# Local attention in a transformer block: the softmax division moved ahead of the transposes, the value product made transposed, and the second half of each tile finished one tile later

## The chip, the cores and the metric

The kernel runs on one core of one Trainium2 chip. The metric is the device time of one execution, in microseconds (us). A core has five engines that each work through a list of instructions in order and wait for each other by semaphores: TensorE (PE in the profile; PEld is its weight load), VectorE (DVE), ScalarE (ACT), GpSimd (POOL) and SyncE (SP, which only issues DMAs here). The on-chip memory SBUF is called `store` in the profile's names, and the eight PSUM banks that TensorE writes are `bank`.

## What is computed

Eight sequences of 512 tokens, 128 wide, pass through four residual blocks: a Mamba-2 block, a two-layer transformer with local attention (call 0), a small attention with distance decay, and the same two-layer transformer again (call 1). The change touches the local attention, which runs four times (2 calls x 2 layers). Its reference, cut to what matters:

```python
q, k, v = split(shift_token(x) @ wqkv)            # 8 heads of 64
q, k = l2norm(q) * qs, l2norm(k) * ksc
q, k = rotary_xpos(q, k)
# windows of 64 queries; each sees its own 64 keys and the 64 before
sim = einsum('bhwid,bhwjd->bhwij', bq * 8, bk)    # masked to a band
attn = softmax(sim)
out = einsum('bhwij,bhwjd->bhwid', attn, bv)
x = x + out @ wo                                  # 512 -> 128
```

After it comes a feed-forward part with a layer norm and a GELU gate.

## The kernel before

**Tiles and stages.** In each layer the eight sequences q are taken one after another, and each is four tiles j of 128 tokens: 32 tiles a layer, 128 in all. A tile passes through a pipeline that is written out by hand, per engine, in a function `attention_sequence`. In the step of tile j, the engines work on several tiles at once:

- TensorE: scores of tile j (`scores`, lines 622 and 629, into banks 3 and 4), the product with the values of tile j-1 (`weigh_values`, 654, into bank 7), the projection of the values of tile j+2 (`project_v`, 600, bank 2), the transposes of the rotated q and k of tile j+1 (`qk_transpose`, 607, banks 5 and 6), the transposes of the attention output of j-1 (`o_transpose`, 662), the transposes of the probabilities (`prob_transpose`, 642, banks 5 and 6), the projection of q and k of tile j+3 (`project_qk`, 593, banks 0 and 1), the output projection of j-1 (`project_out`, 668) and the transpose of an input tile (`x_transpose`, 587).
- VectorE: row maxima (`maxima`, 987), division of the output of j-1 by the sums (`take_o`, 998), the rotary products of tile j+2 (`rotate`, 969 and 974, once for q and once for k), their square sums (981, 983), the reciprocals of the sums (`inverse_sums`, 992), the residual add (`add_out`, 1005).
- ScalarE: squares (822), exponentials of the even and odd heads (`exps`, 844, e = 0 and e = 1), and the copies out of PSUM: values (`copy_v`, 828), q and k (`copy_qkT`, 833 and 835), output (`copy_oT`, 855), probabilities (`copy_pT`, 850).
- GpSimd: adds the two rotary products (`add_turned`, 1134), raises the square sums to the power -1/2 (`inverse_norms`, 1140), and scales q and k (`normalize`, 1149).

**What sets the order.** Nothing but the order of the calls on each engine and the semaphores. Three waits matter below. `project_qk(n, i)` writes bank i and waits on `rot_done` until `rotate` has read tile n-1 out of that bank: the wait is for 8q+2j+i+1 with a credit of 2, so i of tile n needs rotation i of tile n-1. `x_transpose` writes bank 2 and waits on `v_ready` until the values of tile j+2 of this sequence have been copied out of it. `scores` waits on `qT_ready` until both q and k of its tile are copied.

Of the kernel before, what the change touches and what calls it, by code (L numbers as in the profile page):

```python
# [17 lines left out]
ALU = mybir.AluOpType  # L18
# [3 lines left out]
P = 128  # L22
# [115 lines left out]
def hybrid_block(nc, a, out):  # L138
# [3 lines left out]
    with ctx:  # L142
# [52 lines left out]
        onorm = mem.take(INNER)  # L195
        oT = mem.take(PAIRS, P)
        nmax = mem.take(2, PAIRS)
        psums = mem.take(H)
        pinv = mem.take(H)
# [84 lines left out]
        clip_done, pinv_done, fstat_done, feps_done = sem("clip_done"), sem("pinv_done"), sem("fstat_done"), sem("feps_done")  # L284
# [7 lines left out]
        pT_done, pT_ready, o_done, onorm_ready = sem("pT_done"), sem("pT_ready"), sem("o_done"), sem("onorm_ready")  # L292
        oT_done, oT_ready = sem("oT_done"), sem("oT_ready")
# [288 lines left out]
        def transformer_pe(pe, call):  # L582
# [62 lines left out]
            def weigh_values(q, j):  # L645
# [3 lines left out]
                for e in range(2):  # L649
                    pe.wait_ge(pT_ready, n2 + e + 1)  # L650
                    for b in range(PAIRS):
                        h = 2 * b + e
                        for half, v in ((0, VA), (1, V)):
                            last = nc.tensor.matmul(bank[7][half * WIN:(half + 1) * WIN, h * DH:(h + 1) * DH],  # L654
                                                    probT[:, e, b, half * WIN:(half + 1) * WIN], v[:, j, h * DH:(h + 1) * DH],
                                                    start=True, stop=True, skip_group_check=True)
                last.then_inc(o_done, 1)

            def o_transpose(q, j):
                pe.wait_ge(onorm_ready, 4 * q + j + 1)  # L660
                for b in range(PAIRS):
                    last = nc.tensor.transpose(bank[7][:, b * P:(b + 1) * P], onorm[:, b * P:(b + 1) * P], ident)  # L662
                last.then_inc(oT_done, 1)
# [8 lines left out]
            def attention_sequence(q, before, more, ff_ahead=False):  # L672
                for j in range(TPS):
                    prev = (q, j - 1) if j else (q - 1, TPS - 1)
                    has_prev = before or j > 0
# [4 lines left out]
                    if has_prev:  # L680
                        weigh_values(*prev)
                    if more or j < 2:
                        project_v(*((q, j + 2) if j < 2 else (q + 1, j - 2)), more or j == 0)
                    if has_next:
                        qk_transpose(*nxt)
                    if has_prev:
                        o_transpose(*prev)
                    prob_transpose(q, j, 0, has_next)
                    if has_ahead:
                        project_qk(*ahead, 0)  # L690
                    if has_prev:
# [1585 lines left out]
```

## Time and profile before

| what | before |
|---|---|
| median of 3 runs | 2251.19 us (2249.34 to 2251.57) |
| the profiled execution's own time | 2245.52 us |
| its span, first to last instruction | 2243.7 us |
| busy: PE, DVE, ACT, POOL | 95%, 72%, 66%, 75% |
| granted TensorE clock, mean | 0.992 |
| attention stages | 302.9 to about 575 us, 655 to 924, 1545 to 1818, 1898 to 2167 |

A row of the timeline gives start, length, engine, line, operation, and in brackets the idle time just before it and what ended it. Rows are merged when the same line follows itself (x4 is four instructions). An engine takes its next instruction a little before the last one's recorded end, so the distance between starts ("pitch") is a little less than a length.

### The profile page before, as it was taken

The numbers are of one execution on the slowest core, as the hardware profiler recorded it, in microseconds if no ns is written. First come the engines' busy times: TensorE is split into PE (matmuls) and PEld (weight loads), VectorE is DVE, ScalarE is ACT, GpSimd is POOL, SyncE is SP. The second block draws the span as 40 slices with busy tenths as digits, with TensorE's granted clock in tenths as the row PEclk, the third lists the DMA queues.
The fourth block names the chain that finished last, engine by engine and source line by source line (L and its number), as shares of the span: only waits on it lengthen the run. The fifth ranks groups of instructions, "written<-read, shape, count | busy, mean of one in ns | idle before, by whom it ended". The sixth has DMA issues, their size and how long they took to land.

```text
span 2243.7 us, 54540 instructions
## 1 busy us (share of the span) xinstructions
PE 2140.1 (95%) x19744; PEld 1477.6 (66%) x19760; DVE 1613.2 (72%) x3907; ACT 1475.8 (66%) x4130; POOL 1677.2 (75%) x1710
## 2 busy tenths in 40 slices
PE   6999889999999999899999999999999989999998
PEld 4767657777567777556666666565777756777765
DVE  6777568887467777667767777777888756777765
ACT  3666458888458888536656556566888854888862
POOL 7877788998158888448777787778898824888852
PEclk9999989999999999999999999999999999999999
DMA  4000001112111122121111121111111211111211
GB/s 118 1 1 1 7 21 44 35 32 49 48 29 40 33 46 46 43 71 50 49 54 35 48 58 50 44 27 23 42 25 44 46 45 31 37 34 40 47 31 51
DMA packets 121371, 88.42 MB, mean 39 GB/s; under 512 B 85560, under 2 KB 102160, under 8 KB 118800
## 3 DMA queue, kind: packets, MB, share of 16 engines
q1 hardware_dynamic: 118544, 82.69, 15.2%
q8 instruction: 159, 2.61, 0.5%
q10 hardware_dynamic: 2560, 2.24, 0.4%
q14 instruction: 108, 0.88, 0.1%
HBM read 30.38 MB, written 8.39 MB: 17 GB/s over the span
## 4 chain that ended last, share of the span: by engine, by line
PE 65%; DVE 7%; POOL 5%; SPq 5%; issue 3%; DMA 2%; ACT 1%; POOLq 0%; DVEq 0%
PE bank L1328 11%; PE bank L593 8%; PE bank L1339 5%; PE bank L1319 5%; PE bank L607 5%; PE bank L654 4%; PE bank L642 4%; PE bank L629 4%; PE bank L600 4%; PE bank L668 4%; SPq L466 4%; POOL store L1140 3%; PE bank L720 2%; PE bank L662 2%; POOL store L1149 2%
## 5 line engine op out<-in xcount | busy, mean ns | idle before, releaser
L1552 POOL TENSOR_SCALAR store<-store 128x512 f32<-128x512 f32 x512 | 348.7, 693 | 108.2 <-DVE store L1479 106.7
L1479 DVE CUSTOM_DVE_ANT_0 store<-bank,store 128x512 f32<-128x512 f32 x512 | 335.7, 689 | 119.2 <-PE bank L1319 66.8
L1435 ACT ACTIVATE store<-bank 128x512 f32<-128x512 f32 x512 | 286.7, 600 | 201.3 <-PE bank L1328 197.8
L844 ACT ACTIVATE store<-bank,store 128x128 f32<-128x128 f32 x1024 | 362.6, 375 | 69.5 <-DVE store L987 69.4
L1134 POOL TENSOR_TENSOR store<-store 128x512 f32<-128x512 f32 x256 | 320.9, 1275 | 105.7 <-DVE store L974 101.1
L1140 POOL TENSOR_TENSOR store<-store 128x16 f32<-128x16 f32 x128 | 372.5, 2911 | 27.8 <-DVE store L983 27.4
L1328 PEld LDWEIGHTS bank<-store 128*128 128x128 f32 x2048 | 239.7, 141 | 133.1 <-ACT store L1435 75.8
L1328 PE MATMUL bank<-store 128*128 128x128 f32 x2048 | 297.9, 277 | 0.1
L1149 POOL TENSOR_TENSOR store<-store 128x512 f32<-128x512 f32 x256 | 261.5, 1042 | 10.0
L593 PE MATMUL bank<-store 128*128 128x512 f32 x496 | 253.5, 597 | 0.0
L987 DVE TENSOR_REDUCE store<-bank 128x4 f32<-128x512 f32 x256 | 165.0, 686 | 122.9 <-PE bank L629 122.8
L850 ACT ACTIVATE store<-bank 128x512 f32<-128x512 f32 x256 | 157.1, 613 | 113.4 <-PE bank L642 113.4
L844 ACT ACTIVATION_READ_ACCUMULATOR store<-bank,store 128x1 f32 x1024 | 219.3, 214 | 0.0
L720 PE MATMUL bank<-store 128*128 128x512 f32 (+1 forms) x384 | 181.2, 603 | 9.8 <-DVE store L1062 9.8
L607 PEld LDWEIGHTS bank<-store 128*128 128x128 f32 x1024 | 116.6, 141 | 108.9 <-POOL store L1149 75.8
L1319 PE MATMUL bank<-store 72*128 72x512 bf16 x512 | 176.0, 383 | 3.7 <-DVE store L1479 2.5
L668 PEld LDWEIGHTS bank<-store 128*128 128x128 f32 x1024 | 133.1, 191 | 62.1 <-ACT store L855 35.9
L607 PE MATMUL bank<-store 128*128 128x128 f32 x1024 | 155.8, 281 | 16.4 <-POOL store L1149 14.6
L969 DVE TENSOR_TENSOR store<-bank,store 128x512 f32<-128x512 f32 x248 | 169.0, 681 | 2.8 <-ACT store L822 2.8
L642 PEld LDWEIGHTS bank<-store 128*128 128x128 f32 x1024 | 120.7, 141 | 73.3 <-issue 66.2
L974 DVE TENSOR_TENSOR store<-bank,store 128x512 f32<-128x512 f32 x248 | 168.9, 681 | 0.0
L876 ACT ACTIVATE store<-bank,store 128x512 f32<-128x512 f32 (+1 forms) x96 | 65.4, 685 | 151.0 <-PE bank L720 149.4
(220 smaller groups left out, 4442.8 us busy)
## 6 DMA issues: line engine op xcount, KB each, us to landing
store<-store SPq DMA_DIRECT2D x256, 128.0 KB, 2.4
store<-parts SPq DMA_DIRECT2D x96, 192.0 KB
parts<-store SPq DMA_DIRECT2D x16, 384.0 KB, 3.6
store<-store SPq DMA_DIRECT2D x128, 32.0 KB
store<-store SPq DMA_DIRECT2D x128, 31.8 KB
store<-store SPq DMA_DIRECT2D x32, 127.0 KB
store<-in_L_ffn_wqkv_dram SPq DMA_DIRECT2D x4, 768.0 KB, 4.3
out_dram<-store SPq DMA_DIRECT2D x8, 256.0 KB, 2.4
```

The lines of the kernel that those rows point to most:

```text
L593: nc.tensor.matmul(bank[i][:, :], hT[:, j * P:(j + 1) * P], wqkv[:, i * INNER:(i + 1) * INNER], start=True, stop=True).then_inc(qk_done, 1)
L607: last = nc.tensor.transpose(bank[5 + i][:, b * P:(b + 1) * P], roped[:, i, b * P:(b + 1) * P], ident)
L720: nc.tensor.matmul(to, w1[:, half * HID + at:half * HID + at + n], fnT[:, odd, :], start=True, stop=True).then_inc(up_done, 1)
L844: last = nc.scalar.activation(prob[:, e, b, :], bank[3 + e][:, b * P:(b + 1) * P], ACT.Exp, bias=nmax[:, e, b:b + 1], accum_out=psums[:, h ...
L1134: nc.gpsimd.tensor_tensor(straight[:, at, :], straight[:, at, :], turned[:, at, :], ALU.add).then_inc(add_done, 1)
L1140: nc.gpsimd.tensor_tensor(flat, flat, minus_half[:, 0:2 * H], ALU.pow).then_inc(norm_done, 1)
L1149: nc.gpsimd.tensor_tensor(roped[:, i, :].rearrange("p (h d) -> p h d", d=DH), straight[:, at, :].rearrange("p (h d) -> p h d", d=DH), bc(n ...
L1319: nc.tensor.matmul(bank[(64 * q + k) % SCORE_BANKS][:, :], QC[0:COMBO, h, t * P:(t + 1) * P], KC[0:COMBO, h, :], start=True, stop=True).th ...
L1328: last = nc.tensor.transpose(bank[SCORE_BANKS + (64 * q + 4 * h + c) % TURN_BANKS][:, t * P:(t + 1) * P], S[:, h % 4, t, c * P:(c + 1) * P ...
L1435: nc.scalar.activation(AT[:, h % 4, c, :], bank[SCORE_BANKS + (64 * q + 4 * h + c) % TURN_BANKS][:, :], ACT.Exp, scale=-1.0).then_inc(aexp ...
L1479: nc.vector.tensor_tensor_reduce(out=S[:, h % 4, t, :], in0=bank[(64 * q + 4 * h + t) % SCORE_BANKS][:, :], in1=decay[:, off:off + L], sca ...
L1552: nc.gpsimd.tensor_scalar(s_, s_, -1.0, amax[:, h % 4, t:t + 1], ALU.mult, ALU.add).then_inc(shifted_done, 1)
```

## The change

The division by the softmax sums is made on the probabilities themselves, in SBUF, by VectorE (`scale_probs`), once for the even heads (e = 0) and once for the odd, before they are transposed. `take_o` goes. In `weigh_values` the values become the stationary operand and the transposed probabilities the moving one, so that the product comes out transposed, and `o_transpose` goes. The odd half of a tile's probabilities is transposed one tile later, and the output projection and residual add come a further tile later. On TensorE `project_qk` for both q and k now stands ahead of `weigh_values`, and `qk_transpose` behind it. GpSimd's code is as it was.

```diff
@@ transformer_pe
             def prob_transpose(q, j, e, more):
-                pe.wait_ge(exp_done, n2 + e + 3)
+                pe.wait_ge(scaled_p[e], 4 * q + j + 1)
...
-                for e in range(2):
-                    pe.wait_ge(pT_ready, n2 + e + 1)
-                    for b in range(PAIRS):
-                        h = 2 * b + e
-                        for half, v in ((0, VA), (1, V)):
-                            last = nc.tensor.matmul(bank[7][half * WIN:(half + 1) * WIN, h * DH:(h + 1) * DH],
-                                                    probT[:, e, b, half * WIN:(half + 1) * WIN], v[:, j, h * DH:(h + 1) * DH],
+                pe.wait_ge(pT_ready, n2 + 2)
+                for b in range(PAIRS):
+                    for half, v in ((0, VA), (1, V)):
+                        for e in range(2):
+                            h = 2 * b + e
+                            last = nc.tensor.matmul(bank[7][e * DH:(e + 1) * DH, b * P + half * WIN:b * P + (half + 1) * WIN],
+                                                    v[:, j, h * DH:(h + 1) * DH], probT[:, e, b, half * WIN:(half + 1) * WIN],
...
-            def o_transpose(q, j):
...
                     scores(q, j, ff_ahead and j == 0)
                     if has_prev:
-                        weigh_values(*prev)
+                        prob_transpose(*prev, 1, True)
+                    if has_prev2:
+                        project_out(*prev2)
@@ transformer_act
                     exps(q, j, 0)
+                    if has_prev:
+                        copy_pT(*prev, 1)
+                    exps(q, j, 1)
+                    if has_prev:
+                        copy_oT(*prev)
...
@@ transformer_dve
-            def inverse_sums(q, j):
-                dve.wait_ge(exp_done, 8 * q + 2 * j + 4)
-                nc.vector.reciprocal(pinv[:, :], psums[:, :]).then_inc(pinv_done, 1)
-
-            def take_o(q, j):
...
+            def inverse_sums(q, j, e):
+                dve.wait_ge(exp_done, 8 * q + 2 * j + e + 3)
+                nc.vector.reciprocal(pinv[:, e, :], psums[:, e, :]).then_inc(pinv_done[e], 1)
+
+            def scale_probs(q, j, e):
+                dve.wait_ge(pinv_done[e], 4 * q + j + 1)
+                nc.vector.tensor_tensor(prob[:, e, :, :], prob[:, e, :, :], bc(pinv[:, e, :], 2, P), ALU.mult).then_inc(scaled_p[e], 1)
```

TensorE, one tile in the middle of the attention, before (654 product with the values, 600 values of j+2, 607 q and k transposes, 662 output transposes, 642 probability transposes, 593 q and k projections of j+3, 668 output projection):

```order
L654 MATMUL bank<-store 64x64 [waits pT_ready,va_in2,wo_added]
L654 MATMUL bank<-store 64x64 x7
L654 MATMUL bank<-store 64x64 [waits pT_ready]
L654 MATMUL bank<-store 64x64 x7
L600 MATMUL bank<-store 128x512 [waits hT_ready,v_ready]
L607 MATMUL bank<-store 128x128 [waits roped_done]
...
L662 MATMUL bank<-store 128x128 [waits onorm_ready]
...
L642 MATMUL bank<-store 128x128 [waits qT_ready,exp_done]
...
L593 MATMUL bank<-store 128x512 [waits rot_done,hT_ready]
L668 MATMUL bank<-store 128x128 [waits oT_ready]
...
L593 MATMUL bank<-store 128x512 [waits rot_done]
```

The same tile after (lines: 641 probability transposes, 661 output projection, 599 values, 592 q and k projections, 653 product with the values, 606 q and k transposes, 586 input transpose):

```order
L641 MATMUL bank<-store 128x128 [waits qT_ready,scaled_p1]
L641 MATMUL bank<-store 128x128 x3
L661 MATMUL bank<-store 128x128 [waits oT_ready]
L661 MATMUL bank<-store 128x128 x3
L599 MATMUL bank<-store 128x512 [waits hT_ready,v_ready]
L592 MATMUL bank<-store 128x512 [waits rot_done,hT_ready]
L592 MATMUL bank<-store 128x512 [waits rot_done]
L653 MATMUL bank<-store 64x64 [waits pT_ready,va_in0,wo_added]
L653 MATMUL bank<-store 64x64 x15
L606 MATMUL bank<-store 128x128 [waits roped_done]
...
L641 MATMUL bank<-store 128x128 [waits qT_ready,scaled_p0]
L641 MATMUL bank<-store 128x128 x3
L586 MATMUL bank<-store 128x128 [waits v_ready,y_in1]
```

The two projections that wait for `rot_done` have moved from behind the transposes to ahead of the product with the values, and everything behind them in the list stands behind their waits.

VectorE, one tile before:

```order
L987 TENSOR_REDUCE store<-bank 128x4 [waits sim_done] x2
L998 TENSOR_TENSOR store<-bank,store 128x512 [waits pinv_done,o_done]
L969 TENSOR_TENSOR store<-bank,store 128x512 [waits roped_done,sq_done]
L974 TENSOR_TENSOR store<-bank,store 128x512
L969 TENSOR_TENSOR store<-bank,store 128x512 [waits roped_done,sq_done]
L974 TENSOR_TENSOR store<-bank,store 128x512
L981 TENSOR_REDUCE store<-store 128x16 [waits roped_done]
L983 TENSOR_SCALAR store<-store 128x16 [waits ss_done]
L992 RECIPROCAL store<-store 128x8 [waits exp_done]
L1005 TENSOR_TENSOR store<-bank,store 128x128 [waits wo_done]
```

and after (982 maxima, 996 residual add, 964 and 969 the rotary products, 987 reciprocal, 991 the new scaling, 976 and 978 the square sums):

```order
L982 TENSOR_REDUCE store<-bank 128x4 [waits sim_done] x2
L996 TENSOR_TENSOR store<-bank,store 128x128 [waits wo_done]
L964 TENSOR_TENSOR store<-bank,store 128x512 [waits roped_done,sq_done]
L969 TENSOR_TENSOR store<-bank,store 128x512
L987 RECIPROCAL store<-store 128x4 [waits exp_done]
L991 TENSOR_TENSOR store<-store 128x512 [waits pinv_done0]
L964 TENSOR_TENSOR store<-bank,store 128x512 [waits roped_done,sq_done]
L969 TENSOR_TENSOR store<-bank,store 128x512
L976 TENSOR_REDUCE store<-store 128x16 [waits roped_done]
L978 TENSOR_SCALAR store<-store 128x16 [waits ss_done]
L987 RECIPROCAL store<-store 128x4 [waits exp_done]
L991 TENSOR_TENSOR store<-store 128x512 [waits pinv_done1]
```

A reciprocal and a scaling now stand between the two rotations, and the residual add stands ahead of both.

ScalarE's copies, before: values, q, k, output, and then the odd exponentials:

```order
L844 ACTIVATE store<-bank,store 128x128 x3
L828 ACTIVATE store<-bank 128x512 [waits o_done,v_done]
L833 ACTIVATE store<-bank 128x512 [waits qkT_done]
L835 ACTIVATE store<-bank 128x4x128 [waits qkT_done]
L855 ACTIVATE store<-bank 128x512 [waits oT_done]
L844 ACTIVATE store<-bank,store 128x128 [waits pT_done,max_done]
```

and after (836 exponentials, 847 output, 826 and 828 q and k, 821 values, 842 probabilities):

```order
L836 ACTIVATE store<-bank,store 128x128 x3
L847 ACTIVATE store<-bank 128x512 [waits o_done]
L826 ACTIVATE store<-bank 128x512 [waits qkT_done]
L828 ACTIVATE store<-bank 128x4x128 [waits qkT_done]
L821 ACTIVATE store<-bank 128x512 [waits o_done,v_done]
L842 ACTIVATE store<-bank 128x512 [waits pT_done]
```

The copy of the values has moved from first to last of the four, behind a copy that waits for the product with the values.

## Rows read from the trace of the kernel before

**Rows 1.** The page, part 1: busy time, share, instructions of each engine.

```profile
PE 2140.1 (95%) x19744; PEld 1477.6 (66%) x19760; DVE 1613.2 (72%) x3907; ACT 1475.8 (66%) x4130; POOL 1677.2 (75%) x1710
```

**Rows 2.** Timeline, TensorE, one tile: start, length, engine, line, operation, count.

```profile
705.22 0.41 PE L622 MATMUL bank<-store 64*64 64x512 bf16 x4
...
706.43 1.15 PE L654 MATMUL bank<-store 128*64 128x64 f32 x32
...
707.51 1.12 PE L600 MATMUL bank<-store 128*128 128x512 f32 x2
...
709.50 0.60 PE L662 MATMUL bank<-store 128*128 128x128 f32 x4
...
711.23 1.05 PE L668 MATMUL bank<-store 128*128 128x128 f32 x8
...
712.12 1.02 PE L593 MATMUL bank<-store 128*128 128x512 f32 x2
...
712.98 0.60 PE L642 MATMUL bank<-store 128*128 128x128 f32 x4
...
713.42 0.27 PE L587 MATMUL bank<-store 128*128 128x128 f32 x1
...
713.62 0.41 PE L622 MATMUL bank<-store 64*64 64x512 bf16 x4
```

**Rows 3.** Timeline, VectorE, the same tile.

```profile
707.75 0.68 DVE L998 TENSOR_TENSOR store<-bank,store 128x512 f32<-128x512 f32 x1
...
708.35 0.68 DVE L969 TENSOR_TENSOR store<-bank,store 128x512 f32<-128x512 f32 x1
...
708.95 0.68 DVE L974 TENSOR_TENSOR store<-bank,store 128x512 f32<-128x512 f32 x1
...
710.74 1.21 DVE L981 TENSOR_REDUCE store<-store 128x16 f32<-128x1024 f32 x1
...
712.21 0.20 DVE L992 RECIPROCAL store<-store 128x8 f32<-128x8 f32 x1
712.33 0.29 DVE L1005 TENSOR_TENSOR store<-bank,store 128x128 f32<-128x128 f32 x1
```

**Rows 4.** Timeline, ScalarE, the copies of q, k and output in it.

```profile
709.17 0.59 ACT L833 ACTIVATE store<-bank 128x512 f32<-128x512 f32 x1
...
709.70 0.60 ACT L835 ACTIVATE store<-bank 128x512 f32<-128x512 f32 x1
...
710.19 0.59 ACT L855 ACTIVATE store<-bank 128x512 f32<-128x512 f32 x1
```

**Rows 5.** Timeline, GpSimd, the same tile: both adds, then the power.

```profile
709.71 2.51 POOL L1134 TENSOR_TENSOR store<-store 128x512 f32<-128x512 f32 x2 [0.76 <-DVE store L974]
...
712.42 2.91 POOL L1140 TENSOR_TENSOR store<-store 128x16 f32<-128x16 f32 x1 [0.21 <-DVE store L983]
```

**Rows 6.** Timeline, Mamba stage: a GpSimd and a VectorE instruction, both on SBUF only.

```profile
51.58 0.61 POOL L2103 TENSOR_TENSOR store<-store 128x256 f32<-128x256 f32 x1
...
51.65 0.69 DVE L1993 TENSOR_SCALAR store<-store 128x256 f32<-128x256 f32 x1 [0.79 <-POOL store L2127]
58.81 0.35 DVE L1993 TENSOR_SCALAR store<-store 128x256 f32<-128x256 f32 x1 [1.04 <-POOL store L2127]
```

**Rows 7.** Timeline, TensorE: first and 29th tile of the first and second layer.

```profile
302.94 0.41 PE L622 MATMUL bank<-store 64*64 64x512 bf16 x4
...
542.14 0.41 PE L622 MATMUL bank<-store 64*64 64x512 bf16 x4
...
655.08 0.41 PE L622 MATMUL bank<-store 64*64 64x512 bf16 x4
...
891.27 0.41 PE L622 MATMUL bank<-store 64*64 64x512 bf16 x4
```

**Rows 8.** Windows: length, busy PE, PEld, DVE, ACT, POOL; clock, DMA, GB/s.

```profile
264.00:268.00 4.00, 1.21 (x7) 0.81 (x7) 3.65 (x11) 0.38 (x1) 3.78 (x6) 1.00 0.00 0
268.00:272.00 4.00, 4.00 (x11) 2.14 (x11) 0.35 (x1) 0.80 (x3) 2.50 (x6) 0.58 0.01 4
```

More of the change, by code:

```diff
@@ L194, in hybrid_block @@
         probT = mem.take(2, PAIRS, P)
-        onorm = mem.take(INNER)
         oT = mem.take(PAIRS, P)
         nmax = mem.take(2, PAIRS)
-        psums = mem.take(H)
-        pinv = mem.take(H)
+        psums = mem.take(2, PAIRS)
+        pinv = mem.take(2, PAIRS)
         fq = mem.take(2, TPS, P)
@@ L674, in attention_sequence @@
                     prev = (q, j - 1) if j else (q - 1, TPS - 1)
-                    has_prev = before or j > 0
+                    prev2 = (q, j - 2) if j > 1 else (q - 1, j + 2)
+                    has_prev, has_prev2 = before or j > 0, before or j > 1
                     nxt = (q, j + 1) if j < 3 else (q + 1, 0)
@@ L858, in attention_sequence @@
                 for j in range(TPS):
+                    prev, has_prev = (q, j - 1) if j else (q - 1, TPS - 1), before or j > 0
                     if more or j < 2:
@@ L862, in attention_sequence @@
                     exps(q, j, 0)
+                    if has_prev:
+                        copy_pT(*prev, 1)
+                    exps(q, j, 1)
+                    if has_prev:
+                        copy_oT(*prev)
+                    if more or j < 3:
+                        copy_qkT(*((q, j + 1) if j < 3 else (q + 1, 0)))
                     if more or j < 2:
                         copy_v(*ahead)
-                    if more or j < 3:
-                        copy_qkT(*((q, j + 1) if j < 3 else (q + 1, 0)))
-                    if before or j:
-                        copy_oT(*((q, j - 1) if j else (q - 1, TPS - 1)))
-                    exps(q, j, 1)
                     copy_pT(q, j, 0)
-                    copy_pT(q, j, 1)
             def ff_gate(q, i, odd):
@@ L1012, in attention_sequence @@
                         ff_normalize(ff_from, 0, ff_from == 0)
-                    has_prev = before or j > 0
-                    prev = (q, j - 1) if j else (q - 1, TPS - 1)
                     if j and more:
@@ L1020, in attention_sequence @@
                     maxima(q, j, 1)
-                    if has_prev:
-                        take_o(*prev)
+                    if before or j > 1:
+                        add_out(s if j > 1 else s - 1, *((q, j - 2) if j > 1 else (q - 1, j + 2)))
                     if more or j < 2:
@@ L1025, in attention_sequence @@
                         rotate(*ahead, 0)
+                    inverse_sums(q, j, 0)
+                    scale_probs(q, j, 0)
+                    if more or j < 2:
                         rotate(*ahead, 1)
                         square_sums(*ahead)
-                    inverse_sums(q, j)
-                    if has_prev:
-                        add_out(s if j else s - 1, *prev)
+                    inverse_sums(q, j, 1)
+                    scale_probs(q, j, 1)
                     if norm_more and j == 0:
```

40 lines of the change are left out of this document (13 added, 27 removed).

## The prediction

> **What bounds the kernel now.** I read the page's busy shares first: TensorE is busy 95% of the span, GpSimd 75%, VectorE 72%, ScalarE 66% [rows 1]. Then the timeline of one attention tile, engine by engine, since the change touches nothing else. I count from S, the first mask product of the scores of a tile (L622). In [rows 2] S is 705.22 and the next S is 713.62: a tile takes 8.40 us. Over whole layers, the first 28 tiles (seven sequences) take 542.14 - 302.94 = 239.2 us in the first layer and 891.27 - 655.08 = 236.2 us in the second [rows 7]; the third and fourth layer begin and repeat like them, so I take 237.7 us for 28 tiles, 8.49 us each, in four layers.
>
> TensorE is nearly always in work there, so the removed transposes look like pure gain: four of them, 0.60 long, 0.44 to the next start [rows 2]. That holds only as long as nothing else closes a circle within a tile. So I follow, for the new order, what each engine waits for, with these pitches from [rows 2]: scores 706.43 - 705.22 = 1.21; product with the values 1.08; output projection 0.89 (1.05 long); a projection with 512 columns 0.86 (1.02 long); four transposes 0.44.
>
> **The change, part by part.** All times are from S of the tile.
>
> *1. VectorE up to the rotation of q.* The maxima end and the next instruction starts at 707.75 - 705.22 = 2.53 [rows 3]. That next one used to be `take_o`; it is now the residual add of the tile before last. It waits for the output projection, which TensorE reaches behind the scores and one set of transposes: 1.21 + 0.44 + 1.05 = 2.70, plus 0.04 for the hand-over (TensorE's 1.05 from 711.23 ends at 712.28, VectorE's add starts at 712.33), so 2.74. The add is 0.29 long, about 0.20 to the next. The two products of rotation q start at 2.94 and 3.54, 0.60 apart, and the second ends at 4.22.
>
> *2. The first scaling.* Reciprocal from 4.14, 0.20 long [rows 3]; the scaling behind it waits for it, so it can start at about 4.37. GpSimd starts its add on the same rotation: before, 0.76 after the start of L974 (708.95 to 709.71) [rows 3, 5], so now at 4.30, 0.07 ahead of the scaling. It is free by then (below). Both instructions have all operands in SBUF. [Rows 6] show such a pair: GpSimd starts at 51.58, VectorE 0.07 later, and the VectorE instruction takes 0.69 where it takes 0.35 alone; it ends just behind GpSimd's end at 52.19. No row has exactly a two-operand 128x512 in SBUF on VectorE. Bounds: unhindered, the pitch of its relative with one operand in PSUM, 0.60; hindered, until GpSimd's add (2.51 / 2 = 1.25 long) ends at 5.55, plus 0.55. I take the second, because the nearest row has the same 0.07: the rotation of k starts at 6.02 and not at 4.97. The Trainium skill (SBUF — State Buffer, "SBUF: two separate sides") says the same: VectorE with two SBUF inputs and GpSimd take a shared port pair for a whole instruction, and whoever starts first has it; by that rule too the loser waits, and the trace agrees.
>
> *3. The rotation of k, and who waits for it.* It starts at 6.02, and its second product ends at 6.02 + 0.60 + 0.68 = 7.30. Now the moved wait: `project_qk` of tile j+3, half k, may only write bank 1 when this rotation of tile j+2 has read it. Before, that projection came at 712.12 - 705.22 = 6.90 and the rotation had ended by then: no wait. Now TensorE arrives early: scores, transposes, output projection, values end at 1.21 + 0.44 + 0.89 + 0.86 = 3.40, half q waits until about 4.3 for the rotation of q and ends at 5.2, and half k waits until 7.36. Two idle stretches, 0.9 and some 2.1 us, where there were none.
>
> *4. Behind that wait.* Half k, 0.97 with a cold start; the product with the values starts at 8.33 and ends at 9.48 (1.15 long). ScalarE's copy of the output waits for it: 9.52. Then its copies in order, with the pitches of [rows 4] (0.53, 0.49, and 0.48 for the output): q at 10.05 (its transposes end at 10.0), k at 10.59, and last the values at 11.08, 0.60 long, ended at 11.68. `x_transpose` waits for the copy of the values; before, that was made early in the tile. So it starts at 11.75, and the next S follows 0.20 later [rows 2], 0.3 with a cold start: **S' = S + 12.05**.
>
> So the steps from S to S' form one serial chain through VectorE, TensorE and ScalarE, with nothing of the next tile in parallel. A tile costs 12.05 where it cost 8.49.
>
> *5. What does not lengthen it.* The second scaling, behind the square sums: rotation ends 7.30, sum 1.21 long [rows 3], clip behind GpSimd's second add until 8.7, reciprocal, scaling until 9.6 unhindered, and if the power of 2.91 [rows 5] holds it, until 12.4; its user stands at S' + 1.21, so both ends cost nothing. GpSimd: power 8.9 to 11.8, two products of about 1 us, done at 13.9, which is S' + 1.9: free for the add at S' + 4.30. Its 7.5 us of work hide in 12. The squares (ScalarE, next tile) end by S' + 1.2, ahead of the maxima. `inverse_sums` in two halves adds one reciprocal, 0.20, in the chain above. The product with the values in its new form has as many instructions of the same size, 32 in the trace: nothing, and within 0.1 us a tile either way. The removed `take_o` (0.68) and transposes (0.44) are in the chain as taken out. SyncE: its queue holds the same DMAs; the values are copied later, but are used a full tile after that.
>
> *6. Special tiles.* The first tile of a layer has no product of a predecessor: 10.55. The second has no residual add: 11.64. Twenty-six have all. The sum for 28 tiles is 26 x 12.05 + 22.2 = 335.5, against 237.7: +97.8 a layer, **+391** in four. The last sequence has no projections and no values after its second tile, so the waits go; I make its four tiles and the hand-over to the feed-forward part 34 us before and after, 0 +- 3 a layer.
>
> *7. TensorE's clock.* In [rows 8] TensorE was busy 1.21 of 4 us and the next 4 us were granted 0.58 of full: some 3.4 us at the lower level, 1.2 of 2.4 GHz. Just before that fall it had sat idle for 1.84 us, and had only short work before. In the new tile it would be at work some 1.0 of the 4 us up to 7.4. So I expect falls in most tiles, and right ahead of the critical stretch from 7.4 to 9.5 and the transposes behind it. At half speed in 3.4 us up to 1.7 us of work is lost; some of it falls on stretches where TensorE waits anyway. Bounds 0 and 1.7; I take 1.2 a tile, over 27 tiles in four layers: **+130**.
>
> **The sum.** Against the profiled execution: 2245.5 + 391 + 130 = 2767. The median of the runs shown stands 5.7 us above that execution (2251.2 against 2245.5), so about 2770.
>
> **Rivals.**
>
> *The clock stays up.* For it: both idle stretches are short of the 3.5 us of other places. Against it: [rows 8]. Gives 2770 - 130 = 2640.
>
> *VectorE's scaling wins the start.* 0.07 us decide. Then GpSimd's add waits, not the scaling, and the chain is 1.05 shorter: 28 x 4 x 1.05 = 118. With the clock's falls, somewhat fewer: about 2640; without 2525.
>
> *The circle doesn't close (faster).* If the projection asked for a rotation one tile older, or the copy of the values came early enough from another path, TensorE's list would set the tile: 8.49 less 0.44, so 8.05, or GpSimd's 7.5 of work with its gaps, 7.8. It decides from the point where the rotation of k ends before 4.3. Price: 0.44 x 112 = 49 us less, 2202. Against it: the wait's count in the code and the rows' times; VectorE alone needs till 4.97 for the start of that rotation even unhindered.
>
> *A smaller slowdown.* The chain as told, but one or two hand-overs I priced as serial run beside each other, or the last sequence gains: 2350 to 2500.
>
> **How the numbers follow.** Chances: chain with hindered scaling and falling clock 0.52 (2700 to 2830, likeliest 2770); the same with the clock up 0.18 (2640); scaling unhindered 0.16 (2525 to 2640); smaller slowdown 0.08; circle open 0.05 and something near no change 0.01. The range 2520 to 2825 holds the first three nearly in full, some 0.83. Slower than +0.2% 0.94, same 0.01, faster 0.05; 0.2%, about 4.5 us, is what a measurement of this kernel can tell from no change.
>
> **What would show it.** In the profile after: L622 starts 12 to 13.5 us apart; TensorE idle ahead of L592's second instruction, released by VectorE's second product; VectorE's first scaling (L991) near 1.7 us long and the second near 0.7; ScalarE idle ahead of L847, released by TensorE's product; TensorE idle ahead of L586, released by ScalarE's copy of the values; the clock's row under 9 in the attention slices. TensorE's busy share falls to about 80%. Wrong would be: L592 without idle time ahead of it (the circle), L991 at 0.7 in both halves (the start), or clock 9 everywhere with tiles of 12.0.

## The result, and the profile after

The changed kernel takes 2840.63 us (median of 4 runs, 2836.98 to 2843.45) where the kernel before takes 2250.27 on the same chips: 1.263 times as long, 95% interval 1.261 to 1.265. The direction and the mechanism were forecast; the size was not: 2770 us with a range up to 2825 is 71 us short, and the measured time lies outside the range. The profiled execution has a span of 2835.2 us and a mean granted clock of 0.922. One of the four executions of run 1 below had a granted clock of 0.748 and took 3106.94 us; it is left out of every number here.

The page of the changed kernel, parts 1 and 2 (where [rows 1] answer), and the groups of part 5 that the reading rests on. In a group, what stands behind the bar is busy time and mean ns of one, then the idle time just before them and what ended it:

```profile
PE 2342.4 (83%) x19248; PEld 1498.3 (53%) x19248; DVE 1841.5 (65%) x4163; ACT 1477.8 (52%) x4130; POOL 1742.9 (61%) x1710
...
PEclk9999888888998888999999999988888998888899
...
L592 PE MATMUL bank<-store 128*128 128x512 f32 x496 | 364.3, 827 | 319.0 <-DVE store L969 319.0
L1131 POOL TENSOR_TENSOR store<-store 128x16 f32<-128x16 f32 x128 | 430.7, 3365 | 27.7 <-DVE store L978 27.3
...
L847 ACT ACTIVATE store<-bank 128x512 f32<-128x512 f32 x128 | 76.6, 598 | 634.8 <-PE bank L653 634.8
...
L991 DVE TENSOR_TENSOR store<-store 128x512 f32<-128x512 f32 x256 | 306.5, 1197 | 8.7
```

The projection of q and k (L592) sat idle for 319 us until VectorE's rotation released it, and one pass of it took 827 ns on average where it took 597 before (each half, q and k, is two passes; x496 counts passes). ScalarE's copy of the output (L847) waited 635 us for the product with the values. Those are the two waits of the chain. The clock row is under 9 only in slices of the attention.

One tile of the changed kernel, in the timeline, all engines, cut to the chain (it answers [rows 2 to 5]):

```profile
823.39 0.41 PE L621 MATMUL bank<-store 64*64 64x512 bf16 x4
...
826.39 0.68 DVE L964 TENSOR_TENSOR store<-bank,store 128x512 f32<-128x512 f32 x1
...
826.99 0.68 DVE L969 TENSOR_TENSOR store<-bank,store 128x512 f32<-128x512 f32 x1
...
827.75 1.26 POOL L1125 TENSOR_TENSOR store<-store 128x512 f32<-128x512 f32 x1 [3.64 <-DVE store L969]
...
827.79 1.77 DVE L991 TENSOR_TENSOR store<-store 128x512 f32<-128x512 f32 x1
827.82 1.10 PE L592 MATMUL bank<-store 128*128 128x512 f32 x2 [0.81 <-DVE store L969]
...
829.49 0.68 DVE L964 TENSOR_TENSOR store<-bank,store 128x512 f32<-128x512 f32 x1
830.09 0.67 DVE L969 TENSOR_TENSOR store<-bank,store 128x512 f32<-128x512 f32 x1
...
830.82 2.07 PE L592 MATMUL bank<-store 128*128 128x512 f32 x2 [1.90 <-DVE store L969]
...
832.25 0.69 DVE L991 TENSOR_TENSOR store<-store 128x512 f32<-128x512 f32 x1
832.32 3.40 POOL L1131 TENSOR_TENSOR store<-store 128x16 f32<-128x16 f32 x1 [0.21 <-DVE store L978]
832.82 1.55 PEld L653 LDWEIGHTS bank<-store 128*64 128x64 f32 x32 [1.50 <-issue]
832.82 1.69 PE L653 MATMUL bank<-store 128*64 128x64 f32 x32
...
834.55 0.60 ACT L847 ACTIVATE store<-bank 128x512 f32<-128x512 f32 x1 [5.73 <-PE bank L653]
835.13 0.60 ACT L826 ACTIVATE store<-bank 128x512 f32<-128x512 f32 x1
835.62 0.59 ACT L828 ACTIVATE store<-bank 128x512 f32<-128x512 f32 x1
...
836.10 0.60 ACT L821 ACTIVATE store<-bank 128x512 f32<-128x512 f32 x1
...
836.85 0.30 PE L586 MATMUL bank<-store 128*128 128x128 f32 x1 [0.35 <-ACT store L821]
...
837.08 0.41 PE L621 MATMUL bank<-store 64*64 64x512 bf16 x4
```

Read from S = 823.39: rotation of q at 3.00, scaling at 4.40 and 1.77 long, rotation of k at 6.10, its end at 7.37, half k of the projection at 7.43. Up to here every time is within 0.1 of the forecast. Then TensorE is slow: half k is 2.07 long where half q of the same size took 1.10, and the product with the values takes 1.69 where it took 1.15. The copy of the output starts at 11.16 and not at 9.52, and S' is 13.69 and not 12.05. The windows of those two stretches show the granted clock (columns: the stretch, its length, busy time and count of PE, PEld, DVE, ACT and POOL, granted clock, DMA share, GB/s):

```profile
830.82:832.80 1.98, 1.98 (x2) 0.50 (x2) 1.91 (x4) 0.00 (x0) 1.75 (x2) 0.50 0.00 0
832.80:834.40 1.60, 1.60 (x33) 1.55 (x32) 0.15 (x1) 0.00 (x0) 1.60 (x1) 0.62 0.00 0
```

0.50 is the lower level, 1.2 GHz. It falls in every steady tile, at the end of the 1.90 us in which TensorE waited for the rotation or up to 1.1 us behind it. In the first, second and fourth layer the place is the same in every tile (half k 2.07 long). In the third the fall first comes behind half k (1.12 long in the third tile) and moves forward from tile to tile, until half k is 2.08 long in the 25th; those tiles take 13.67 to 13.80 us, so the place matters little there.

### The profile page after: what moved, and what is told of

The parts are those of the page before. It is cut to its first block, busy times and chain, and to the rows that moved or that the text cites. A ratio compares the mean times of both kernels' runs of the same rounds, so it can differ in the third digit from the quotient of the medians.

```text
span 2835.2 us, 53660 instructions
## 1 busy us (share of the span) xinstructions
PE 2342.4 (83%) x19248; PEld 1498.3 (53%) x19248; DVE 1841.5 (65%) x4163; ACT 1477.8 (52%) x4130; POOL 1742.9 (61%) x1710
## 4 chain that ended last, share of the span: by engine, by line
PE 51%; DVE 15%; issue 10%; ACT 8%; SPq 3%; DMA 1%; POOL 1%; POOLq 0%; DVEq 0%
PE bank L1319 8%; PE bank L592 8%; PE bank L653 7%; DVE store L964 6%; DVE store L969 5%; PE bank L1330 4%; PE bank L628 4%; PE bank L1310 4%; PE bank L661 4%; PE bank L641 3%; PE bank L712 2%; SPq L465 2%; ACT store L821 2%; ACT store L828 2%; ACT store L847 2%
## 5 line engine op out<-in xcount | busy, mean ns | idle before, releaser
L592 PE MATMUL bank<-store 128*128 128x512 f32 x496 | 364.3, 827 | 319.0 <-DVE store L969 319.0
L1131 POOL TENSOR_TENSOR store<-store 128x16 f32<-128x16 f32 x128 | 430.7, 3365 | 27.7 <-DVE store L978 27.3
L847 ACT ACTIVATE store<-bank 128x512 f32<-128x512 f32 x128 | 76.6, 598 | 634.8 <-PE bank L653 634.8
L1426 ACT ACTIVATE store<-bank 128x512 f32<-128x512 f32 x512 | 286.8, 600 | 202.1 <-PE bank L1319 198.6
L592 PEld LDWEIGHTS bank<-store 128*128 128x128 f32 x496 | 93.6, 234 | 513.9 <-DVE store L969 316.1
L957 DVE COPY store<-bank 128x128 f32<-128x128 f32 x120 | 34.4, 291 | 440.3 <-PE bank L586 440.3
L991 DVE TENSOR_TENSOR store<-store 128x512 f32<-128x512 f32 x256 | 306.5, 1197 | 8.7
L1319 PEld LDWEIGHTS bank<-store 128*128 128x128 f32 x2048 | 240.5, 142 | 133.6 <-ACT store L1426 75.8
L1319 PE MATMUL bank<-store 128*128 128x128 f32 x2048 | 298.8, 277 | 0.0
L653 PEld LDWEIGHTS bank<-store 128*64 128x64 f32 x4096 | 192.4, 193 | 182.0 <-issue 178.8
L982 DVE TENSOR_REDUCE store<-bank 128x4 f32<-128x512 f32 x256 | 164.8, 686 | 134.1 <-PE bank L628 134.1
L653 PE MATMUL bank<-store 128*64 128x64 f32 x4096 | 210.9, 281 | 20.2 <-ACT store L842 17.8
L641 PE MATMUL bank<-store 128*128 128x128 f32 x1024 | 167.8, 287 | 43.8 <-ACT store L826 37.0
L964 DVE TENSOR_TENSOR store<-bank,store 128x512 f32<-128x512 f32 x248 | 168.4, 679 | 2.8 <-ACT store L815 2.8
```

Of the source, the lines that this page charges most:

```text
L592: nc.tensor.matmul(bank[i][:, :], hT[:, j * P:(j + 1) * P], wqkv[:, i * INNER:(i + 1) * INNER], start=True, stop=True).then_inc(qk_done, 1)
L653: last = nc.tensor.matmul(bank[7][e * DH:(e + 1) * DH, b * P + half * WIN:b * P + (half + 1) * WIN], v[:, j, h * DH:(h + 1) * DH], probT[: ...
L964: nc.vector.tensor_tensor(straight[:, at, :].rearrange("p (h d) -> p h d", d=DH), bank[i][:, :].rearrange("p (h d) -> p h d", d=DH), bc(ro ...
L991: nc.vector.tensor_tensor(prob[:, e, :, :], prob[:, e, :, :], bc(pinv[:, e, :], 2, P), ALU.mult).then_inc(scaled_p[e], 1)
L1131: nc.gpsimd.tensor_tensor(flat, flat, minus_half[:, 0:2 * H], ALU.pow).then_inc(norm_done, 1)
L1319: last = nc.tensor.transpose(bank[SCORE_BANKS + (64 * q + 4 * h + c) % TURN_BANKS][:, t * P:(t + 1) * P], S[:, h % 4, t, c * P:(c + 1) * P ...
```

## The experiments

Times of a tile are distances between the first mask products of two tiles, as in [rows 7], in the steady part of a layer. Runs 2, 3, 5, 6, 8 and 9 have one time each; the others are medians of several, and the interval stands with the ratio. All of them compute everything unless the expectation says what is left out.

**1. TensorE kept at work in the idle stretch.**

```diff
                         project_qk(*ahead, 0)
+                        if has_prev2:
+                            pe.wait_ge(wo_added, 4 * prev[0] + prev[1] + 1)
+                            for _ in range(2):
+                                nc.tensor.matmul(bank[7][:, :], ident, wqkv[:, 0:INNER], start=True, stop=True)
                         project_qk(*ahead, 1)
```

> The changed kernel, with two more fp32 products of 512 columns on TensorE between the two halves of the q and k projection; their result (in bank 7) is used by nobody. They lie in the stretch from 5.4 to 7.4 us of a tile in which TensorE waits for VectorE's rotation of k. Theory (the 1.64 us that a tile is longer than the 12.05 us of the chain are TensorE's lower clock behind that idle stretch): the granted clock stays at its upper level in the attention, the half k of the projection takes 1.1 us again and not 2.07, and a tile falls from 13.66 to about 12.1 us; time about 2840 - 108 x 1.6 = 2665 us. Rival (the clock has nothing to do with it, the moved instructions are slower for another reason): a tile stays at 13.66 us or grows by what of the 1.7 us does not fit into the stretch, 2840 us or more.

Measured: 2681.51 us, 1.193 (1.191 to 1.195) of before: 159 us less than the changed kernel, for more work, and 17 us over what was expected. A tile takes 12.21 us. The timeline of this run, the fill (L685) and what follows:

```profile
839.86 1.10 PE L592 MATMUL bank<-store 128*128 128x512 f32 x2 [0.81 <-DVE store L973]
...
840.79 1.88 PE L685 MATMUL bank<-store 128*128 128x512 f32 x4
...
842.86 1.13 PE L592 MATMUL bank<-store 128*128 128x512 f32 x2 [0.19 <-DVE store L973]
...
843.92 1.15 PE L653 MATMUL bank<-store 128*64 128x64 f32 x32
```

Half k waits for the same release at the same place of the tile, but takes 1.13, and the product 1.15; the mean granted clock of the execution is 0.987. So the clock's fall is real, and it costs 13.66 - 12.21 = 1.45 us in a steady tile. The rival, that the moved instructions are slow for another reason, is out.

**2 and 3. The scaling without GpSimd in its way.** The even scaling takes its second operand from PSUM (the division of the even heads is so left out); with two fill products, and with one.

```diff
-nc.vector.tensor_tensor(prob[:, e, :, :], prob[:, e, :, :], bc(pinv[:, e, :], 2, P), ALU.mult)
+nc.vector.tensor_tensor(prob[:, e, :, :], prob[:, e, :, :],
+    bc(pinv[:, e, :], 2, P) if e else bank[3][:, :].rearrange("p (b w) -> p b w", w=P), ALU.mult)
```

> As the run with two more products, and besides the scaling of the even heads takes its second operand from PSUM (the scores) and not the reciprocals from SBUF; the division of the even heads is so left out, the instruction has the same size and place. Theory (the scaling is 1.77 us long because GpSimd's add, started 0.04 us ahead of it, keeps it from SBUF): it takes 0.68 us, the rotation of k starts 1.07 us earlier, and a tile falls from about 12.1 to about 11.0 us: 118 us less than the other, about 2550 us. Rival (the 1.77 us is the price of the instruction with its broadcast operand and in-place output): it stays near 1.7 us and the tile at 12.1.

Measured: 2607.97 us, a tile of 11.76 us. Timeline of this run:

```profile
838.93 1.27 POOL L1130 TENSOR_TENSOR store<-store 128x512 f32<-128x512 f32 x1 [2.76 <-DVE store L973]
838.97 0.69 DVE L995 TENSOR_TENSOR store<-store,bank 128x512 f32<-128x512 f32 x1
...
839.58 0.68 DVE L968 TENSOR_TENSOR store<-bank,store 128x512 f32<-128x512 f32 x1
```

Same start, 0.04 behind GpSimd's add, and 0.69 long instead of 1.77: with one operand in PSUM it runs beside the add. The instruction itself is as expected, the time was not: 74 us less instead of 118. The rotation of k now ended 1.1 us earlier, but TensorE was still at the fill products and had no idle time ahead of half k. That was my own addition becoming the wait, so the next run has one of them less.

> As the run with two more products and the even scaling's second operand in PSUM (division of the even heads left out), but with one more product on TensorE instead of two. In that run a tile took 11.76 us, because the two products ended at 7.08 us of the tile and the rotation of k, now earlier, at 6.29. Theory (the scaling's wait for GpSimd costs the chain 1.09 us, and 0.6 of it was hidden by the second product): with one product the half k of the projection starts at 6.35, a tile takes 11.1 to 11.2 us, and the time is about 2540 us (2682 less 28 x 4 x 1.1, and some more at the layers' ends). Rival (the wait's cost is only the 0.46 us a tile seen there): a tile stays at 11.7 us, 2605 us.

Measured: 2545.43 us, a tile of 11.13 us. The hindrance costs the chain 12.21 - 11.13 = 1.08 us, where the prediction priced 1.05.

**4. The projections back behind the product with the values.**

```diff
-                    if has_ahead:
-                        project_qk(*ahead, 0)
-                        project_qk(*ahead, 1)
                     if has_prev:
                         weigh_values(*prev)
                     if has_next:
                         qk_transpose(*nxt)
+                    if has_ahead:
+                        project_qk(*ahead, 0)
+                        project_qk(*ahead, 1)
                     prob_transpose(q, j, 0, has_next)
```

> The changed kernel with TensorE's order changed in one point: both halves of the q and k projection stand behind the product with the values and the transposes of q and k, not ahead. Theory (the projections' wait for the rotation, placed ahead of the product with the values, closes the circle): the product with the values starts 4.1 us after the first scores instead of 9.4, the copies follow, the wait for the rotation of k hides behind it, TensorE keeps its clock; a tile takes 9.0 to 9.3 us, time about 2345 us (2310 to 2390). That is still slower than the kernel before, since the first half of the projection's work behind the rotation and the scaling's wait remain. Rival (VectorE's longer list with its waits is what makes the tile long, wherever TensorE waits): a tile stays above 12 us, 2640 us or more.

Measured: 2301.10 us, 1.024 (1.022 to 1.025) of before, a little under the expected span (and so is the tile). This one move gives back 540 of the 590 us. A tile takes 8.82 us, 9.63 in every fourth of the first and third layer. The moved wait named in the prediction's step 3 was needed for nearly all of the slowdown. Timeline, GpSimd and VectorE in one tile of this run:

```profile
833.41 1.55 DVE L991 TENSOR_TENSOR store<-store 128x512 f32<-128x512 f32 x1
...
834.38 3.14 POOL L1125 TENSOR_TENSOR store<-store 128x512 f32<-128x512 f32 x2
...
837.66 0.69 DVE L991 TENSOR_TENSOR store<-store 128x512 f32<-128x512 f32 x1
837.73 3.40 POOL L1131 TENSOR_TENSOR store<-store 128x16 f32<-128x16 f32 x1 [0.21 <-DVE store L978]
```

GpSimd has no idle time but for 0.21, and two of its instructions are longer than in [rows 5]: the two adds 3.14 instead of 2.51, the power 3.40 instead of 2.91. My theory for what is left of the slowdown was GpSimd kept out of SBUF by the scalings.

**5. The same order, and the even scaling's second operand in PSUM** (run 4 with the edit of run 2).

> The run with the projections moved behind the product with the values, and besides the even scaling's second operand in PSUM (division of the even heads left out). In that run a tile took 8.82 us and GpSimd was never idle but for 0.2 us: two adds 3.14 us together where they took 2.51 before, the power 3.40 where it took 2.91, two products 2.04. Theory (GpSimd's list sets that tile, and VectorE's scalings lengthen it by keeping GpSimd out of SBUF): the two adds take 2.5 us again, the power stays at 3.4 (the odd scaling is as it was), a tile takes 8.2 to 8.4 us and the time falls by 45 to 65 us, to 2235 to 2255. Rival (TensorE's or ScalarE's list sets it): 8.8 us and 2300 us as before.

Measured: 2254.57 us, at the upper end; a tile of 8.56 us. The adds on their own:

```profile
857.78 1.28 POOL L1126 TENSOR_TENSOR store<-store 128x512 f32<-128x512 f32 x1
859.38 1.27 POOL L1126 TENSOR_TENSOR store<-store 128x512 f32<-128x512 f32 x1 [0.32 <-DVE store L969]
860.87 3.39 POOL L1132 TENSOR_TENSOR store<-store 128x16 f32<-128x16 f32 x1 [0.21 <-DVE store L978]
```

They are 1.28 long again, and the time falls by 47 us, to within 0.3% of before. But the second add now waits 0.32 for the rotation of k, because the scaling still stands between the two rotations. By my reckoning, not tried, that wait is why a tile did not come to 8.4: GpSimd is idle nowhere else but for 0.21.

**6. The values copied first.**

```diff
                     exps(q, j, 1)
+                    if more or j < 2:
+                        copy_v(*ahead)
                     if has_prev:
                         copy_oT(*prev)
```

(and the call removed from behind `copy_qkT`).

> The changed kernel with ScalarE's order changed in one point: the copy of the values stands ahead of the copy of the output, as first of the four. Theory (the four copies behind the product with the values are in series in the tile's chain): the last of the chain is then the copy of k, the next scores start about 0.55 us earlier, and a tile takes 13.1 us; time about 2780 us. Rival (TensorE's clock falls once in every tile at the same place, and the tile's length settles where it does): the tile stays at 13.66 us although its chain is shorter, 2840 us.

Measured: 2720.26 us, neither of the two. Tiles of 11.67 us alternate with one to three of 12.8 to 13.25, 12.6 to 12.7 in the mean. The 11.67 us tiles are those in which the clock didn't fall: 12.21 - 11.67 = 0.54 is the copy's share of the chain, as expected. In the others it falls, and not always at the same place, as here, where half k is still fast and the product and the transposes of q and k behind it are slow (1.77 and 1.97 for 1.15 and 1.09):

```profile
830.80 1.13 PE L592 MATMUL bank<-store 128*128 128x512 f32 x2 [1.91 <-DVE store L969]
...
831.86 1.77 PE L653 MATMUL bank<-store 128*64 128x64 f32 x32
...
833.56 1.97 PE L606 MATMUL bank<-store 128*128 128x128 f32 x8
```

Against those tiles a fall costs 1.1 to 1.6 us here, by where in the tile it comes, and 31 of the 104 steady tiles have none; that, beside the 0.54, is where the time under both expectations comes from. In the changed kernel the clock fell in all 26 steady tiles of a layer. Why the shorter tile escapes now and then, with the same waits of 0.81 and 1.90 us, no run here shows.

**7. The two rotations together again, the rest as changed.** The reciprocal and scaling of the even heads stand behind `square_sums` on VectorE; TensorE and ScalarE keep the changed order.

> The changed kernel with VectorE's order changed in one point: the reciprocal and scaling of the even heads stand behind the square sums, so that the two rotations follow each other again; TensorE's and ScalarE's order are the changed kernel's. Theory (the rotation of k ends 1.9 us earlier, at 5.4 of the tile, the second idle stretch of TensorE is gone and with it the fall of its clock; the projections still stand ahead of the product with the values, and the four copies behind it): a tile takes 10.0 to 10.2 us for 13.66, the time is 2440 to 2475 us. Rival (the clock falls all the same, or the later scaling becomes the wait of the even probabilities' transposes): a tile of 11 us or more, 2550 us or more.

Measured: 2446.33 us, 1.088 (1.086 to 1.090) of before, a tile of 10.32 us, 0.1 over the expected span of a tile, and the time inside. Timeline:

```profile
857.79 2.23 PE L592 MATMUL bank<-store 128*128 128x512 f32 x4 [0.81 <-DVE store L969]
...
859.96 1.15 PE L653 MATMUL bank<-store 128*64 128x64 f32 x32
```

Both halves of the projection now follow each other (four passes in 2.23), the wait of 1.90 has gone and the wait of 0.81 alone brings no fall: mean granted clock 0.995. So two thirds of the slowdown, 394 us, came from one scaling between two rotations, through three terms. The tile is 13.66 - 10.32 = 3.34 us shorter: 1.45 for the clock (run 1), 1.08 for the scaling's wait for GpSimd (runs 2 and 3), and the 0.81 left for the reciprocal and scaling themselves (0.20 and 0.60 to the next start, as priced). The 394 us do not add to the 540 of run 4: the moved projections and the scaling between the rotations each make the other dearer, and taking back either removes the cost that they share.

**8 and 9. The removals alone.** The kernel before, product transposed, output transposes gone, division left out.

> The kernel before with one part of the change alone: the product with the values made transposed, and the transposes of the output gone. The division by the sums is left out altogether (neither on the product nor on the probabilities). This bounds from above what the change could bring by its removals. Theory (TensorE's list is nearly full and the rotations also start 0.6 us earlier, so that GpSimd is no wait): a tile takes 8.0 to 8.1 us for 8.49, the time is 2251 - 112 x 0.45 = 2200 us (2185 to 2215). Rival (another circle, over ScalarE's copies, keeps the tile at 8.4): 2240 to 2250 us.

Measured: 2314.16 us, slower than before and outside both expectations. A tile takes 9.15 us. Timeline of this run, then of the one after it:

```profile
854.61 1.90 PE L654 MATMUL bank<-store 128*64 128x64 f32 x32
...
856.44 1.13 PE L600 MATMUL bank<-store 128*128 128x512 f32 x2
```

The product with the values (16 products in the code, 32 records in the trace) takes 1.83 us to the next start where it took 1.08 [rows 2]. The count and size are those of before. What differs is which half of the array's columns each uses: I had left the loop over even and odd heads outermost, so 16 records in a row go to one half; in the kernel before, and in the changed one, they alternate. The next run alternates them:

```diff
-                for e in range(2):
-                    for b in range(PAIRS):
-                        for half, v in ((0, VA), (1, V)):
+                for b in range(PAIRS):
+                    for half, v in ((0, VA), (1, V)):
+                        for e in range(2):
```

> The run with the kernel before, the product transposed and the division left out, once more, with one difference: the 32 small products of a tile alternate between the two halves of the array's columns (even head, odd head) as the changed kernel's do; in the first such run 16 in a row went to the same half. There they took 1.83 us to the next instruction, in every other kernel 1.08, and a tile 9.15 us. Theory (products that follow each other on different halves of the columns run beside each other, on the same half they don't): they take 1.08 again and the tile is 0.75 shorter, 8.4 us, about 2314 - 112 x 0.75 = 2230 us; the removed output transposes and division then bring only about 0.1 us a tile, because TensorE waits for ScalarE's copy of q instead. Rival (the values as stationary operand are what costs): 1.83 and 9.15 us stay, 2314 us.

Measured: 2232.31 us, a tile of 8.40 us.

```profile
854.29 1.15 PE L654 MATMUL bank<-store 128*64 128x64 f32 x32
...
855.38 1.12 PE L600 MATMUL bank<-store 128*128 128x512 f32 x2
...
857.03 0.59 ACT L830 ACTIVATE store<-bank 128x512 f32<-128x512 f32 x1
...
857.77 0.63 PE L642 MATMUL bank<-store 128*128 128x128 f32 x4 [0.39 <-ACT store L830]
```

1.09 to the next start, as the expectation's theory has it, and 82 us less than run 8. And the removals, with the division for nothing, bring 17 us in the order of before: the probabilities' transposes (L642) now wait 0.39 for ScalarE's copy of q (L830), which swallows the 0.44 of the removed transposes. Most of the gain stands in the first and third layer (4.6 and 4.5 us for 28 tiles; 1.7 each in the other two), where tiles of 9.04 fell to 8.40.

**10. The parts of the change in an order without the circle.** TensorE: scores, both halves of the last tile's probabilities, output projection, values, half q, product with the values, transposes of q and k, half k, input. VectorE: rotation q, residual add, rotation k, square sums, both reciprocals, both scalings. ScalarE: probabilities' copies around the even exponentials, values ahead of the output.

```diff
+                        prob_transpose(*prev, 0, True)
                         prob_transpose(*prev, 1, True)
...
                         project_qk(*ahead, 0)
-                        project_qk(*ahead, 1)
                     if has_prev:
                         weigh_values(*prev)
                     if has_next:
                         qk_transpose(*nxt)
-                    prob_transpose(q, j, 0, has_next)
+                    if has_ahead:
+                        project_qk(*ahead, 1)
```

> The changed kernel's parts in another order, complete in its computation. TensorE: scores, both halves of the probabilities of the tile before, output projection, values, half q of the projection, product with the values, transposes of q and k, half k, input. VectorE: both rotations and the square sums ahead of both scalings, which so fall beside GpSimd's power and start behind it. ScalarE: values ahead of the output, both copies of probabilities around the even exponentials. Theory (what made the change slow is the order of the waits, not its operations): TensorE needs 7.75 us, ScalarE 7.8, GpSimd 7.75, VectorE 7.2 us a tile; a tile takes 7.9 to 8.2 us and the time is 2190 to 2225 us, faster than before. Rival (with all four engines nearly full, hand-overs add up): a tile of 8.5 us or more, 2250 us or more.

Measured: 2217.01 us, 0.986 (0.984 to 0.987) of before, the fastest of all here and complete. A tile takes 8.06 us in the second and fourth layer, and 8.06 to 9.25 in the first and third.

```profile
PE 2089.7 (94%) x19232; PEld 1401.4 (63%) x19248; DVE 1786.3 (81%) x4163; ACT 1470.6 (66%) x4130; POOL 1731.2 (78%) x1710
...
858.28 1.28 DVE L982 TENSOR_SCALAR store<-store 128x16 f32<-128x16 f32 x1
...
859.68 1.31 DVE L995 TENSOR_TENSOR store<-store 128x512 f32<-128x512 f32 x2
859.75 3.40 POOL L1135 TENSOR_TENSOR store<-store 128x16 f32<-128x16 f32 x1 [0.21 <-DVE store L982]
```

VectorE is at work 81% of the span, and some of that is waiting for GpSimd inside its instructions (L982, a clip of 16 columns, is 1.28 long here and 0.2 in the tile before). Which engine now sets the tile is not shown: in two tiles of this stretch TensorE has no idle time, GpSimd 0.21 us and VectorE 0.23. That VectorE sets it, and that its layer-norm work is what lengthens tiles in the first and third layer, is my reading, not tried.

## Why the prediction was wrong, point by point

- **Steps 1 to 4, the chain**, were right place by place. Without the clock's falls a steady tile takes 12.21 (run 1) for 12.05. The sum of 28 tiles is 342 us there and not 335.5: four times 6.4, 26 us. Of these, 17 are small hand-overs in the 26 steady tiles. The rest stands in the first two tiles of a layer, 24.2 us together for the forecast 22.2: run 1 has no fill products there, and in six of these eight tiles the granted clock fell too (in the first layer 0.50 from 310 to 312 us and again from 324 to 326), so this part belongs to step 7.
- **Step 2, the start decided by 0.07 us**, went as taken; the scaling starts 0.04 us behind the add and is 1.77 long. The rival that it wins is out, and its price, 1.05, was 1.08 (runs 2 and 3).
- **Step 3, the moved wait** is confirmed by run 4: 540 us for one move.
- **Step 5, no cost elsewhere**: right for the changed kernel, where the longer power (3.37 us in the mean for 2.91) hides in GpSimd's idle time. It stops being free once the chain is short, as run 4 shows.
- **Step 6, the last sequence and the hand-over at 0 +- 3 us** was under-sized. From the first tile of the first layer to that of the second are 352.1 us before (655.08 - 302.94) and 499.6 after (798.73 - 299.17), 147.4 more, of which 28 tiles give 141.7; the rest, 5.7 a layer, 23 us, lies behind the 28th tile. The four layers together agree: the spans less 4 x 28 tiles are 1292.4 us before (2243.7 - 951.3) and 1315.3 after (2835.2 - 1519.9). The first tile of the last sequence still has the last projections, and with them the whole chain and the clock's fall: 13.0 us for 8.3. The third waits for its late second half (1.08 us for the odd scaling, 2.45 for the copy of those probabilities) and takes 10.4 for 8.3. The second takes 7.3 for 7.8.
- **Step 7, the clock**, is the third mis-sized term, and with the other two it put the time outside the range. I took 1.2 us a tile between 0 and 1.7; it is 1.45 in every steady tile, because the fall always comes where what follows it on TensorE is in the chain (in the tile above half k has 2.00 to the next start for 1.06 in run 1, and the product with the values 1.62 for 1.08). From run 1 to the changed kernel that is 38 us a layer on 28 tiles, 152 us for 130.

So the steps that failed are three terms of the sum, each too small, and no link of the mechanism: 26 + 23 + 22 = 71 us, which is what 2841 is over 2770. The range was made of the rivals and of the bounds of the clock alone: its upper end, 2825, took every other term of the dearest case at its middle value. The case held likeliest is the one that came, 11 us above its own span (2700 to 2830); the width around it was too small.

## What to carry to other kernels

When an instruction moves ahead of others on an in-order engine, take along every wait that it has, and ask what in the same step releases it: here a wait that had 1.3 us of slack (the rotation of k ended at 710.82, its projection began at 712.12) closed a circle through three engines and made the tile 60% longer, while the removed work was worth 17 us in the old order. Add the bounds of all terms to the range, not of the uncertain one alone, and price a new idle stretch of TensorE at what the lower clock costs in the work behind it. Once the circle is known, the same operations in another order can still gain (1.4% here).

## What the runs showed of the hardware that I had not expected

- Two more products a tile made a kernel faster by 159 us, because TensorE then kept its upper clock. The clock fell behind waits of 0.81 and 1.90 us separated by one projection, and did not where only the 0.81 was left. In the changed kernel it falls once in every steady tile, in three of the layers always at the same place and in the third layer at a place that moves forward by some 1.3 us in 24 tiles; after a small change of the tile's length (run 6) it falls in some tiles and not in others, at changing places.
- The 16 products of 64 columns (32 records) take 1.08 us when they alternate between the two halves of the array's columns and 1.83 us when 16 records in a row use one half (runs 9 and 8, the same products in another order).
- GpSimd and VectorE keep each other out of SBUF in both directions, by some hundredths of a us in the start: 0.04 behind GpSimd's add, a scaling takes 1.77 for 0.69; 0.07 ahead of GpSimd's power, it makes the power 3.40 for 2.91. Step 2 of the prediction took the wait to last for the other's whole instruction. For the adds it did; for the power it does not: in run 7 a second scaling starts inside it, at 850.87 against the power's 850.12, and takes 0.69:

```profile
850.05 0.69 DVE L991 TENSOR_TENSOR store<-store 128x512 f32<-128x512 f32 x1
850.12 3.40 POOL L1131 TENSOR_TENSOR store<-store 128x16 f32<-128x16 f32 x1 [0.21 <-DVE store L978]
...
850.87 0.69 DVE L991 TENSOR_TENSOR store<-store 128x512 f32<-128x512 f32 x1
```
